# A MoE down-projection: three bfloat16 matmuls per chunk, or one in float32

## The chip, the cores and the metric

The kernel runs on one NeuronCore of a Trainium2 chip. Its engines run side by side, each with its own in-order instruction stream, and wait for each other on semaphores: TensorE (matmuls, from SBUF into PSUM), VectorE, ScalarE, GpSimd, and SyncE, which here only issues transfers. In the profile they are PE, DVE, ACT, POOL and SP; PEld is TensorE's weight load. The metric is the device time of one execution in microseconds (us); less is better.

## The reference

The input is 128 images of 64 x 64 pixels with 128 channels, all float32. A depthwise 3 x 3 convolution and an 8 x 8 mean pool make 64 tokens of 128 numbers from each. Then follow, each added to its input and each on a normalised copy of it: an attention over the 64 tokens of an image, a mixture of experts, a second attention with compressed keys, and a small MLP over the tokens. The change is in the mixture of experts, of which this is the core (`t` holds the tokens, D = 128, F = 512, 2 shared experts and 8 routed ones; the routing gives each token two of these, but all eight are computed and weighted):

```python
hs = gelu(einsum('td,nfd->ntf', t, sw1) + sb1[:, None, :])
shared = einsum('ntf,ndf->td', hs, sw2) + sb2.sum(axis=0)
probs = softmax(t @ gate_w.T + gate_b)
top_v, top_i = top_k(probs, 2)
cw = zeros_like(probs).at[arange(T)[:, None], top_i].add(top_v)
hr = gelu(einsum('td,efd->etf', t, rw1) + rb1[:, None, :])
oe = einsum('etf,edf->etd', hr, rw2) + rb2[:, None, :]
return shared + einsum('etd,te->td', oe, cw)
```

The Gelu is the exact one.

## The kernel before

The images are worked in 16 groups of 8, that is, of 512 tokens. Four stages are pipelined over the groups: `tok` (convolution and pooling), `att` (first attention and routing), `ffn` (the experts) and `sec` (second attention and MLP). Iteration i runs `tok` of group i, `att` of group i-1, `ffn` of i-2 and `sec` of i-3. So iterations 0 to 2 fill the pipeline, 16 to 18 drain it, and those between do all four stages. Twelve of the iterations run as a hardware loop with two iterations in its body; at its end every engine jumps back.

The order of the work on each engine is written out by hand in the table `ORDER`: one string per engine, whose words are pieces such as `up.12`, `pool.3.2` or `att.12`. A word with a prime (`down.38'`) belongs to the iteration before. `iteration` walks through the string and emits each piece with its waits, so every engine executes just this order and a piece that has to wait holds up all that stand behind it.

**The experts.** There are 10 experts with 4 chunks of 128 hidden units each, 40 chunks a group. For chunk q:
- `up.q` on TensorE (L490 to L492) puts the pre-activation [128 x 512 tokens] into one of two banks. Float32 accuracy comes from three bfloat16 products: high times high, low times high, high times low, where high is the value in bfloat16 and low the rest.
- `hidden.q` on ScalarE (L732) takes the Gelu twice from the same bank: once into the bfloat16 tile `hid_h`, once into the float32 tile `hid`.
- `hidden.q` on VectorE (L991), or on GpSimd (L1141) for every fifth chunk, subtracts the two and writes the low part `hid_l`.
- `down.q` on TensorE (L505 to L507) waits for that subtraction (`rest_taken`) and adds three bfloat16 products into `down_bank`, which the four chunks of an expert share (the two shared experts' eight chunks, for the first sum).
- `sum.q` on VectorE (L1001, L1008) takes the bank at an expert's end, with the bias and the token's share of this expert, and GpSimd (L1148) adds it to `moe`. The next expert's first `down` waits for the `sum`.

`hid_h` and `hid_l` are rings of 5 chunks, `hid` a ring of 4. For each routed expert one more matmul (L485) spreads the tokens' shares over the partitions, and ScalarE copies them (L721).

**What lies around it.** `pair` and `inner` on VectorE (L878, L882), `add` on GpSimd (L1133) and `pool` on TensorE (L410, L413, L418) are the pooling of an x tile, `tap` the convolution's 15 steps (L899, the last ones L906), and `out` turns the result (L382). `att.11` computes the routing logits, GpSimd their exponential (L1123), and `att.12` on VectorE is the routing: a chain of 14 dependent small operations (L956 to L986). `low` (L941) splits the normalised tokens into high and low parts, once a group. `turn` and `value` (L575, L584, and L1062 and L1065 on VectorE) are parts of the second attention, `k` in L870 is written by `att.10`.

**Weights.** In iteration 1 all of w1 and w2 (10 slices each of 128 x 512) come in through four staging tiles: GpSimd issues the transfer, ScalarE writes the high part (L657), VectorE the low part (L851). These are the pieces `weights.0` to `weights.19`. The constants come on ScalarE's queue at the start (L637, L639), and each engine waits for all of them at the start of iteration 1.

Of the kernel before, what the change touches and what calls it, by code (L numbers as in the profile page):

```python
# [19 lines left out]
P = 128  # L20
# [17 lines left out]
HIDS = 4  # L38
STAGING = 4
POOL_EVERY = 5  # L40
# [12 lines left out]
        up.0 up.1 down.38' down.39' up.2 up.3 down.0 down.1 up.4 att.1 pool.0.0 pool.0.1 up.5 pre.0 down.2  # L53
        up.6 att.2 down.3 up.7 down.4 att.3 down.5 up.8 down.6 pre.2 pool.0.2 pool.0.3 up.9 up.10 att.4 pre.3
        up.11 down.7 pre.4 up.12 down.8 pre.5 pre.6 pool.1.0 up.13 pool.1.1 down.9 pre.7 up.14 up.15 score.0
        score.1 down.10 down.11 score.2 score.3 up.16 down.12 up.17 pool.1.2 down.13 up.18 down.14 up.19
        pool.1.3 down.15 score.4 up.20 score.5 score.6 down.16 score.7 down.17 up.21 down.18 down.19 up.22
        pool.2.0 pool.2.1 att.7 turn.0 down.20 up.23 turn.1 value.0 att.8 turn.2 value.1 down.21 turn.3
        value.2 up.24 pool.2.2 turn.4 up.25 pool.2.3 down.22 up.26 value.3 down.23 turn.5 att.10 value.4 up.27
        turn.6 value.5 att.11 turn.7 value.6 up.28 value.7 up.29 post.0 down.24 post.1 up.30 down.25 down.26  # L60
        down.27 up.31 pool.3.0 down.28 pool.3.1 up.32 up.33 pool.3.2 pool.3.3 down.29 up.34 att.13 down.30
        up.35 down.31 post.3 up.36 post.4 down.32 up.37 up.38 down.33 down.34 down.35 up.39 post.5 down.36
        down.37 out""",
# [4 lines left out]
        pool.1.0 hidden.13 pre.7 hidden.14 weights.9 hidden.15 inner.1.1 hidden.16 hidden.17 pool.1.2  # L68
        hidden.18 hidden.19 pool.1.3 weights.10 weights.11 hidden.20 weights.12 inner.2.0 att.6 exp hidden.21
        turn.0 weights.13 att.7 weights.14 hidden.22 turn.1 turn.2 hidden.23 pool.2.0 inner.2.1 turn.3  # L70
        hidden.24 hidden.25 turn.4 hidden.26 turn.5 att.10 inner.3.0 turn.6 weights.15 hidden.27 turn.7
        hidden.28 post.0 weights.16 hidden.29 weights.17 hidden.30 pool.2.2 pool.2.3 pool.3.0 hidden.31
        inner.3.1 hidden.32 weights.18 pool.3.2 pool.3.3 hidden.33 hidden.34 hidden.35 post.3 att.13 hidden.36
        hidden.37 post.4 weights.19 hidden.38 hidden.39 post.5 out""",
    dve="""
        pair.0.0 hidden.38' att.0 hidden.0 weights.0 sum.39' hidden.1 att.1 inner.0.0 weights.1 hidden.2
        hidden.3 weights.2 pair.0.1 pre.0 pre.1 hidden.5 hidden.6 pre.2 weights.3 hidden.7 inner.0.1 weights.4
        pair.1.0 pre.5 pre.3 sum.7 weights.5 hidden.8 pre.4 inner.1.0 hidden.10 att.4 pair.1.1 weights.6
        hidden.11 hidden.12 hidden.13 att.5 score.0 weights.7 score.1 sum.11 weights.8 score.2 inner.1.1
        hidden.15 score.3 hidden.16 weights.9 pair.2.0 hidden.17 hidden.18 weights.10 sum.15 tap.0.0 score.4  # L80
        tap.0.1 score.5 tap.0.2 score.6 weights.11 tap.0.3 score.7 tap.0.4 inner.2.0 hidden.20 tap.0.5 sum.19
# [32 lines left out]
def program(nc, x, conv_w, conv_b, wq, bq, wk, bk, gate_w, gate_b, w1, b1, w2, sb2, rb2,  # L114
            swq, swqs, swk, swks, swv, swkc, swvc, swo, comp_gate, sink, tw1, tb1, tw2, tb2,
            ident_c, block_c, cos_c, sin_c, mask1_c, limit_c, place_c, part_c, heads_c, pick_c, tie_c, out):
    with ExitStack() as ctx:
# [174 lines left out]
        def rest_taken(g, q):  # L292

            if q % POOL_EVERY == POOL_EVERY - 1:
                return hid_rest_p, at(hid_rest_p, g, q // POOL_EVERY + 1)
            return hid_rest, at(hid_rest, g, q + 1 - q // POOL_EVERY)


        first = [q + max(0, q // FC - NS + 1) for q in range(CH)]
        def made(n):  # L300
# [968 lines left out]
```

## Time and profile before

| | |
|---|---|
| Median of 3 runs | 2192.52 us (2187.37 to 2193.03) |
| Profiled execution, its own time | 2185.65 us |
| Its span, first to last instruction | 2183.9 us |
| Mean granted TensorE clock in it | 0.956 of 2.4 GHz |
| TensorE busy | 1868.5 us (86%) |
| VectorE busy | 1880.1 us (86%) |
| ScalarE busy | 1331.7 us (61%) |
| GpSimd busy | 1207.4 us (55%) |

Busy time is the time in which an engine had an instruction in work. For TensorE it says less than for the others, since matmuls overlap and the end of each is modelled: the distance from one start to the next tells what a matmul costs in a row of them. An idle stretch is put down to what ended it ("<- DVE part L1008"), and "issue" is time in which the engine waited for nothing that the profile shows. Idle time costs something only on the engine that sets the pace.

### The profile page before, as it was taken

How to read it: one execution, taken by the hardware profiler on the slowest of the kernel's cores; microseconds unless marked ns; L12 is line 12 of the kernel's file. 1: busy time of each engine (PE TensorE's matmuls, PEld its weight loads, DVE VectorE, ACT ScalarE, POOL GpSimd, SP SyncE). 2: the span in 40 equal slices, each digit the busy share in tenths (PEclk: the TensorE clock that was granted, in tenths of full speed). 3: DMA queues.
4: the chain of work that ended last, by engine and by line, in shares of the span. 5: the costliest groups of instructions: out<-in, count | busy, mean ns of one | idle time of the engine just before them, and what ended most of it. 6: DMA issues, size and time to landing. Idle time of an engine off the chain costs nothing.

```text
span 2183.9 us, 38353 instructions
## 1 busy us (share of the span) xinstructions
PE 1868.5 (86%) x12224; PEld 1066.0 (49%) x12224; DVE 1880.1 (86%) x3524; ACT 1331.7 (61%) x2319; POOL 1207.4 (55%) x796
## 2 busy tenths in 40 slices
PE   2355889898988989798998989888998989899986
PEld 2344545455454545455454555545454555544444
DVE  1667899999999999899998989989998989987762
ACT  0234767666675766567675757657675756768752
POOL 1244557574755657575663757466565647554532
PEclk9999999999999999899998989999998989999996
DMA  5664534243343434334333424333343433200000
GB/s 181 250 241 183 193 123 155 114 159 151 121 160 117 155 121 155 122 145 165 121 129 137 155 94 160 150 122 150 125 155 112 164 122 124 109 6 1 5 6 5
DMA packets 33616, 282.00 MB, mean 129 GB/s; under 512 B 5470, under 2 KB 15649, under 8 KB 17020
## 3 DMA queue, kind: packets, MB, share of 16 engines
q1 hardware_dynamic: 18432, 268.44, 32.1%
q10 hardware_dynamic: 13372, 5.66, 0.9%
q0 software_dynamic: 1600, 5.24, 0.6%
q8 instruction: 112, 1.84, 0.3%
q14 instruction: 100, 0.82, 0.1%
HBM read 275.14 MB, written 4.19 MB: 128 GB/s over the span
## 4 chain that ended last, share of the span: by engine, by line
PE 40%; DVE 35%; issue 16%; DMA 2%; POOL 2%; ACT 2%; ACTq 1%; DVEq 1%; POOLq 0%
DVE taps L899 7%; DVE hid_l L991 7%; DVE xbuf L878 5%; PE pool_bank L413 4%; PE hid_bank L490 3%; PE down_bank L505 3%; PE hid_bank L492 3%; PE hid_bank L491 3%; PE down_bank L507 2%; PE down_bank L506 2%; PE sec_bank L528 2%; PE pool_bank L418 2%; PE sec_bank L544 2%; DMA xbuf<-in_x 2%; DVE k L870 2%
## 5 line engine op out<-in xcount | busy, mean ns | idle before, releaser
L732 ACT ACTIVATE hid_h<-hid_bank,b_s 128x512 bf16<-128x512 f32 x640 | 439.3, 686 | 280.9 <-PE hid_bank L492 221.9
L991 DVE TENSOR_TENSOR hid_l<-hid,hid_h 128x512 bf16<-128x512 f32 x512 | 498.3, 988 | 21.3 <-ACT hid L732 20.9
L1133 POOL TENSOR_TENSOR xbuf<-xbuf 128x512 f32<-128x512 f32 x256 | 359.8, 1405 | 266.1 <-DVE xbuf L878 257.2
L732 ACT ACTIVATE hid<-hid_bank,b_s 128x512 f32<-128x512 f32 x640 | 437.3, 683 | 0.0
L1141 POOL TENSOR_TENSOR hid_l<-hid,hid_h 128x512 bf16<-128x512 f32 x128 | 201.1, 1571 | 201.7 <-ACT hid L732 201.7
L1148 POOL TENSOR_TENSOR moe<-moe,part 128x512 f32<-128x512 f32 x128 | 196.6, 1536 | 179.9 <-DVE part L1008 178.1
L490 PE MATMUL hid_bank<-x2h,w1h 128*128 128x512 bf16 x640 | 253.8, 396 | 28.6 <-issue 17.7
L505 PE MATMUL down_bank<-hid_h,w2h 128*128 128x512 bf16 x640 | 252.5, 395 | 27.2 <-DVE part L1008 20.4
L899 DVE SCALAR_TENSOR_TENSOR taps<-pooled_s,tapw,taps 128x256 f32<-128x256 f32 (+1 forms) x416 | 269.6, 648 | 3.5
L878 DVE TENSOR_TENSOR xbuf<-xbuf 128x1536 f32<-128x1536 f32 x128 | 229.8, 1795 | 32.0 <-DMA xbuf<-in_x 23.6
L491 PE MATMUL hid_bank<-x2h,w1l 128*128 128x512 bf16 x640 | 250.9, 392 | 0.0
L492 PE MATMUL hid_bank<-x2l,w1h 128*128 128x512 bf16 x640 | 250.5, 391 | 0.0
L506 PE MATMUL down_bank<-hid_h,w2l 128*128 128x512 bf16 x640 | 250.4, 391 | 0.0
L507 PE MATMUL down_bank<-hid_l,w2h 128*128 128x512 bf16 x640 | 249.8, 390 | 0.0
L1175 POOL TENSOR_TENSOR keys_h<-keys,heads 128x632 f32<-128x632 f32 x128 | 206.9, 1640 | 4.7 <-PE sec_bank L564 3.4
L410 PE MATMUL pool_bank<-block_b,xbuf 128*128 128x48 bf16 x1024 | 50.5, 191 | 133.7 <-DVE xbuf L882 92.4
L413 PE MATMUL pool_bank<-block_sum,xbuf 128*128 128x48 f32 x1024 | 161.9, 308 | 0.0
L676 ACT ACTIVATE pooled_s<-pool_bank 128x384 f32<-128x384 f32 x192 | 90.4, 491 | 115.0 <-PE pool_bank L413 110.4
L1114 POOL TENSOR_TENSOR rs<-ve,power 128x4 f32<-128x4 f32 x64 | 80.8, 1262 | 139.0 <-DVE ve L865 136.4
L418 PEld LDWEIGHTS pool_bank<-block_sum,xbuf 128*128 128x128 f32 x1024 | 143.9, 211 | 11.2 <-issue 1.0
L413 PEld LDWEIGHTS pool_bank<-block_sum,xbuf 128*128 128x128 f32 x1024 | 148.1, 223 | 0.0
L418 PE MATMUL pool_bank<-block_sum,xbuf 128*128 128x48 f32 x1024 | 142.4, 288 | 0.0
(180 smaller groups left out, 3329.3 us busy)
## 6 DMA issues: line engine op xcount, KB each, us to landing
xbuf<-in_x SPq DMA_DIRECT2D x128, 2048.0 KB, 7.3
out<-h ACTq DMA_DIRECT2D x16, 256.0 KB, 2.2
hid<-in_w POOLq DMA_DIRECT2D x10, 256.0 KB, 4.4
part<-in_w POOLq DMA_DIRECT2D x10, 256.0 KB, 6.4
keys_h<-in_limit_c ACTq DMA_DIRECT2D x1, 167.5 KB
tw_s<-in_tw ACTq DMA_DIRECT2D x2, 64.0 KB
share_b<-in_pick_c ACTq DMA_DIRECT2D x1, 96.0 KB
ident<-in_ident_c ACTq DMA_DIRECT2D x1, 64.0 KB, 12.2
```

The costliest lines, as they stand in the source:

```text
L413: mm = nc.tensor.matmul(view[:, 1, :, side[bx]], blocks[v][:, bx, 0, :], block_sum[:], start=True, stop=True)
L418: mm = nc.tensor.matmul(view[:, :, v, side[bx]], blocks[v][:, bx, 7, :], block_sum[:], start=True, stop=True)
L490: nc.tensor.matmul(bank[:], w1h[:, e, cols], x2h[b][:], start=True, stop=False)
L491: nc.tensor.matmul(bank[:], w1l[:, e, cols], x2h[b][:], start=False, stop=False)
L492: nc.tensor.matmul(bank[:], w1h[:, e, cols], x2l[b][:], start=False, stop=True).then_inc(hid_done, 1)
L505: nc.tensor.matmul(down_bank[:], w2h[:, e, cols], hid_h[:, r, :], start=begin, stop=False)
L506: nc.tensor.matmul(down_bank[:], w2l[:, e, cols], hid_h[:, r, :], start=False, stop=False)
L732: nc.scalar.activation(dst[:, r, :], hid_bank[n % 2][:], ACT.Gelu, bias=b1_s[:, q:q + 1]) \
L878: nc.vector.tensor_tensor(v[:, :, 1:6:2, :], v[:, :, 1:6:2, :], v[:, :, 2:7:2, :], ALU.add) \
L899: nc.vector.scalar_tensor_tensor(dst, src, w, dst, ALU.mult, ALU.add).then_inc(tapped, 1)
L991: nc.vector.tensor_tensor(hid_l[:, q % RING, :], hid[:, q % HIDS, :], hid_h[:, q % RING, :], ALU.subtract).then_inc(hid_rest, 1)
L1133: nc.gpsimd.tensor_tensor(v[:, :, 1, :], v[:, :, 1, :], v[:, :, 2 * k + 3, :], ALU.add) \
```

## The change

Down becomes one native float32 matmul per chunk, `hid` times `w2_s`, both float32. The second Gelu and the tiles `hid_h` and `hid_l` go, with the subtractions on VectorE and GpSimd; `hid` becomes a ring of 5. `down.q` waits for the Gelu itself (`hid_made`). The weights w2 are no longer split: they come as they are in one transfer of 128 x 5120 float32 (2.6 MB), the last of the constants on ScalarE's queue, and the pieces `weights.10` to `weights.19` are gone. From `ORDER` only the words `hidden.*` of VectorE and GpSimd and those ten `weights.*` are taken out; the rest stands in the same order, and TensorE's string has the same words as before.

```diff
-HIDS = 4
 STAGING = 4
-POOL_EVERY = 5
 RING = 5
...
     dve="""
-        pair.0.0 hidden.38' att.0 hidden.0 weights.0 sum.39' hidden.1 att.1 inner.0.0 weights.1 hidden.2
+        pair.0.0 att.0 weights.0 sum.39' att.1 inner.0.0 weights.1 weights.2 pair.0.1 pre.0 pre.1 pre.2 weights.3
...
-        w2h, w2l = sb("w2h", [P, NX, F], bf16), sb("w2l", [P, NX, F], bf16)
+        w2_s = sb("w2_s", [P, NX, F])
...
-        hid = sb("hid", [P, HIDS, F])
-        hid_h, hid_l = sb("hid_h", [P, RING, F], bf16), sb("hid_l", [P, RING, F], bf16)
+        hid = sb("hid", [P, RING, F])
...
-                 (tb1_s, tb1), (tb2_s, tb2)]
+                 (tb1_s, tb1), (tb2_s, tb2), (w2_s, w2)]
...
-        lots = [(w1, w1h, w1l, e) for e in range(NX)] + [(w2, w2h, w2l, e) for e in range(NX)]
+        lots = [(w1, w1h, w1l, e) for e in range(NX)]
...
-                eng.wait_ge(*rest_taken(g, q))
+                eng.wait_ge(hid_made, at(hid_made, g, first[q] + 1))
...
-                nc.tensor.matmul(down_bank[:], w2h[:, e, cols], hid_h[:, r, :], start=begin, stop=False)
-                nc.tensor.matmul(down_bank[:], w2l[:, e, cols], hid_h[:, r, :], start=False, stop=False)
-                nc.tensor.matmul(down_bank[:], w2h[:, e, cols], hid_l[:, r, :], start=False, stop=end) \
+                nc.tensor.matmul(down_bank[:], w2_s[:, e, cols], hid[:, r, :], start=begin, stop=end) \
                   .then_inc(hid_used, 1)
...
-                if q >= HIDS:
-                    eng.wait_ge(*rest_taken(g, q - HIDS))
-                elif after(g, 1):
-                    eng.wait_ge(*rest_taken(g - 1, CH + q - HIDS))
-                for dst, r in ((hid_h, q % RING), (hid, q % HIDS)):
-                    nc.scalar.activation(dst[:, r, :], hid_bank[n % 2][:], ACT.Gelu, bias=b1_s[:, q:q + 1]) \
-                      .then_inc(hid_made, 1)
+                nc.scalar.activation(hid[:, q % RING, :], hid_bank[n % 2][:], ACT.Gelu, bias=b1_s[:, q:q + 1]) \
+                  .then_inc(hid_made, 1)
...
-            def hidden(g, q):
-
-                eng.wait_ge(hid_made, at(hid_made, g, made(first[q] + 1)))
-                nc.vector.tensor_tensor(hid_l[:, q % RING, :], hid[:, q % HIDS, :], hid_h[:, q % RING, :],
-                                        ALU.subtract).then_inc(hid_rest, 1)
```

How it moves the instructions is seen best on TensorE and VectorE. First TensorE before, with down.25, down.26 and down.27, then up.31 (L490 to L492):

```order
L505 MATMUL down_bank<-hid_h,w2h 128x512 [waits hid_rest]
L506 MATMUL down_bank<-hid_h,w2l 128x512
L507 MATMUL down_bank<-hid_l,w2h 128x512
L505 MATMUL down_bank<-hid_h,w2h 128x512 [waits hid_rest]
L506 MATMUL down_bank<-hid_h,w2l 128x512
L507 MATMUL down_bank<-hid_l,w2h 128x512
L505 MATMUL down_bank<-hid_h,w2h 128x512 [waits hid_rest]
L506 MATMUL down_bank<-hid_h,w2l 128x512
L507 MATMUL down_bank<-hid_l,w2h 128x512
L490 MATMUL hid_bank<-x2h,w1h 128x512 [waits hid_made]
L491 MATMUL hid_bank<-x2h,w1l 128x512
L492 MATMUL hid_bank<-x2l,w1h 128x512
```

The same place after, where the down matmul is L481 and up is L466 to L468:

```order
L481 MATMUL down_bank<-hid,w_s 128x512 [waits hid_made] x3
L466 MATMUL hid_bank<-x2h,w1h 128x512 [waits hid_made]
L467 MATMUL hid_bank<-x2h,w1l 128x512
L468 MATMUL hid_bank<-x2l,w1h 128x512
L386 MATMUL pool_bank<-block_b,xbuf 128x3x16 [waits pooled_read,inner_low,x_in0]
L386 MATMUL pool_bank<-block_b,xbuf 128x3x16 x7
L389 MATMUL pool_bank<-block_sum,xbuf 128x3x16 x4
```

Nine down matmuls in bfloat16 became three in float32, and they wait for the Gelu (`hid_made`) instead of the subtraction (`hid_rest`).

VectorE before, from the shared experts' `sum.7` (L1001) to the row maximum of the first attention (L925):

```order
L1001 TENSOR_SCALAR moe<-down_bank,sb_sum 128x512 [waits moe_turned,hid_used]
L991 TENSOR_TENSOR hid_l<-hid,hid_h 128x512 [waits hid_made]
L1035 TENSOR_TENSOR keys_h<-sec_bank,cos 128x512 [waits rope_added,rope_done]
L1035 TENSOR_TENSOR keys_h<-sec_bank,sin 128x512 [waits rope_done]
L882 TENSOR_TENSOR xbuf<-xbuf 128x4x128 [waits inner_high]
L991 TENSOR_TENSOR hid_l<-hid,hid_h 128x512 [waits hid_made]
L921 TENSOR_TENSOR s<-att_bank,mask 128x512 [waits s1_done]
L878 TENSOR_TENSOR xbuf<-xbuf 128x4x3x128 [waits x_in1]
L991 TENSOR_TENSOR hid_l<-hid,hid_h 128x512 [waits hid_made] x3
L925 TENSOR_REDUCE nmax<-s 128x4 [waits s1_masked]
L1054 TENSOR_REDUCE m<-sec_bank 128x4 [waits scored]
```

And after, from the same `sum.7` (now L964), with the maximum at L894:

```order
L964 TENSOR_SCALAR moe<-down_bank,sb_sum 128x512 [waits moe_turned,hid_used]
L995 TENSOR_TENSOR keys_h<-sec_bank,cos 128x512 [waits rope_added,rope_done]
L995 TENSOR_TENSOR keys_h<-sec_bank,sin 128x512 [waits rope_done]
L851 TENSOR_TENSOR xbuf<-xbuf 128x4x128 [waits inner_high]
L890 TENSOR_TENSOR s<-att_bank,mask 128x512 [waits s1_done]
L847 TENSOR_TENSOR xbuf<-xbuf 128x4x3x128 [waits x_in1]
L894 TENSOR_REDUCE nmax<-s 128x4 [waits s1_masked]
L1014 TENSOR_REDUCE m<-sec_bank 128x4 [waits scored]
```

Five subtractions are gone from between, and what stood behind them moves up in the same order.

## Rows read from the trace of the kernel before

**Rows 1.** Page, part 1: engine, busy us, share of the span, instructions.
```profile
PE 1868.5 (86%) x12224; PEld 1066.0 (49%) x12224; DVE 1880.1 (86%) x3524; ACT 1331.7 (61%) x2319; POOL 1207.4 (55%) x796
```

**Rows 2.** Timeline of VectorE, its `low` pieces: start us, us, engine, line, operation.
```profile
192.53 0.69 DVE L941 TENSOR_TENSOR x2l<-x1t,x2h 128x512 bf16<-128x512 f32 x1
...
288.23 0.69 DVE L941 TENSOR_TENSOR x2l<-x1t,x2h 128x512 bf16<-128x512 f32 x1
...
1908.59 0.69 DVE L941 TENSOR_TENSOR x2l<-x1t,x2h 128x512 bf16<-128x512 f32 x1
```

**Rows 3.** Busy time by windows: length, busy us (instructions) of each engine, clock, DMA.
```profile
288.20:1908.60 1620.40, 1475.43 (x9923) 831.98 (x9922) 1520.86 (x2822) 1064.49 (x1858) 985.53 (x624) 0.96 0.36 136
1167.64:1296.74 129.10, 117.55 (x764) 66.52 (x764) 116.32 (x218) 81.87 (x143) 75.19 (x49) 0.92 0.35 134
1296.74:1419.57 122.83, 112.52 (x764) 63.71 (x764) 117.14 (x218) 81.99 (x143) 76.16 (x49) 0.97 0.37 140
1921.89:2019.76 97.87, 91.93 (x567) 45.83 (x568) 72.94 (x172) 72.05 (x123) 47.33 (x32) 1.00 0.01 4
2019.76:2108.66 88.90, 86.29 (x525) 40.76 (x524) 60.12 (x117) 66.77 (x108) 39.21 (x30) 1.00 0.01 4
```

**Rows 4.** Waits of TensorE, 288.2 to 1908.6 us: total us, times, longest.
```profile
PE pool_bank L410 <- DVE xbuf L882: 41.6, 13, 3.4
PE pool_bank L382 <- DVE cols L906: 24.3, 13, 1.9
PE down_bank L505 <- DVE part L1008: 18.1, 36, 1.2
PE hid_bank L490 <- issue: 17.7, 5, 3.7
PE sec_bank L584 <- DVE x L1065: 13.3, 13, 1.0
PE att_bank L382 <- DVE k L870: 12.9, 13, 1.0
```

**Rows 5.** Page, part 5: groups: busy us, mean ns, idle before.
```profile
L991 DVE TENSOR_TENSOR hid_l<-hid,hid_h 128x512 bf16<-128x512 f32 x512 | 498.3, 988 | 21.3 <-ACT hid L732 20.9
...
L732 ACT ACTIVATE hid<-hid_bank,b_s 128x512 f32<-128x512 f32 x640 | 437.3, 683 | 0.0
L1141 POOL TENSOR_TENSOR hid_l<-hid,hid_h 128x512 bf16<-128x512 f32 x128 | 201.1, 1571 | 201.7 <-ACT hid L732 201.7
```

**Rows 6.** Timeline of TensorE, around three down chunks.
```profile
1015.58 0.38 PE L505 MATMUL down_bank<-hid_h,w2h 128*128 128x512 bf16 x1
...
1017.52 0.38 PE L490 MATMUL hid_bank<-x2h,w1h 128*128 128x512 bf16 x1
```

**Rows 7.** Timeline of TensorE, float32 matmuls of 512 columns.
```profile
2035.20 1.02 PE L528 MATMUL sec_bank<-x3t,second_q 128*128 128x512 f32 x2
2036.06 1.02 PE L528 MATMUL sec_bank<-x3t,second_qs 128*128 128x512 f32 x2
2036.91 0.38 PE L490 MATMUL hid_bank<-x2h,w1h 128*128 128x512 bf16 x1
```

**Rows 8.** Groups by shape, weight loads.
```profile
L528 PEld LDWEIGHTS sec_bank<-x3t,second_qs 128*128 128x128 f32 x32 | 6.4, 199 | 8.2 <-issue 8.2
```

**Rows 9.** Timeline of VectorE, around the routing chain.
```profile
1018.88 0.75 DVE L1008 SCALAR_TENSOR_TENSOR part<-down_bank,rb_s,share_b 128x512 f32<-128x512 f32 x1
1019.54 0.18 DVE L956 TENSOR_REDUCE esum<-ez 128x4 f32<-128x32 f32 x1
...
1026.61 0.69 DVE L882 TENSOR_TENSOR xbuf<-xbuf 128x512 bf16<-128x512 f32 x1
```

**Rows 10.** Timeline of TensorE, the wait behind it.
```profile
1027.43 0.37 PE L410 MATMUL pool_bank<-block_b,xbuf 128*128 128x48 bf16 x8 [3.37 <-DVE xbuf L882]
```

**Rows 11.** Page, part 6: DMA issues: KB each, us to landing.
```profile
xbuf<-in_x SPq DMA_DIRECT2D x128, 2048.0 KB, 7.3
```

**Rows 12.** Groups by shape, VectorE, the low parts of w2.
```profile
L851 DVE TENSOR_TENSOR w2l<-part,w2h 128x512 bf16<-128x512 f32 x6 | 4.1, 687 | 1.7 <-ACT w2h L657 1.7
```

## What I predict, before the run

> **What bounds the kernel now.** I read the page's first part, then the busy time by windows, then the waits of TensorE, then the timelines of TensorE and VectorE around the longest of these waits.
>
> The page shows two engines at 86%, TensorE and VectorE [rows 1]. The steady part runs from one `low` piece (L941) at 288.23 us to another at 1908.59 us [rows 2]; 13 periods lie between, so a period is 1620.4/13 = 124.65 us. In it VectorE is busy 1520.86/13 = 117.0 us, TensorE 1475.43/13 = 113.5, ScalarE 81.9, GpSimd 75.8 [rows 3]. VectorE has 7.6 us left, most of it in gaps between dependent instructions: it is the saturated engine. TensorE idles 11.15 us in a period. 127.9 of its 145 us of idle time have a name in six groups, and five of them, 110.2 us, end on VectorE [rows 4]. So VectorE sets the pace and TensorE is close behind: whatever takes load from the first and gives it to the second ends on TensorE soon. The granted clock is 0.96 in this stretch, that is, part of it is spent at 1.2 GHz instead of 2.4. A period without the loop's jump shows 0.97 and 112.52 us of TensorE, one with the jump 0.92 and 117.55 [rows 3]: one point of clock is worth about 5.03/5 = 1.0 us of TensorE's busy time.
>
> **What goes.** Of VectorE, the 512 `hid_l` subtractions: 498.3 us, 31.1 in each of the 16 groups. Of ScalarE, one of two Gelu per chunk: 437.3 us, 27.3 a group. Of GpSimd, 128 subtractions, 201.1 us, 12.6 a group [rows 5]. A period's loads become 117.0 - 31.1 = 85.9 us on VectorE, 54.6 on ScalarE, 63.2 on GpSimd. None of it is worth its own size: these three engines stop being the bound, and TensorE has only 11.15 us of idle time to give.
>
> **What comes.** Each down chunk was three bfloat16 matmuls of 512 columns. Three chunks in a row start at 1015.58 and the next work at 1017.52, which is 1.94/3 = 0.647 us a chunk [rows 6]. (A record's own 0.38 is longer than its slot of 0.215, since its end is modelled 0.165 behind.) A float32 matmul of the same shape stands in the trace as two records; two such matmuls start at 2035.20 and 2036.06, and the next work at 2036.91: 0.855 to 0.86 each [rows 7]. So a chunk costs 0.86 - 0.647 = 0.213 us more, 8.5 us a group of 40 chunks, 136 us over 16 groups at the full clock, and twice that where the clock is at 1.2 GHz.
>
> The float32 weight loads take 199 ns on average [rows 8], and each of the two pairs of rows 7 runs at 0.43 us a record with its load inside. The Trainium skill, "TensorE: Matmul & The Clock Gate", section "Weight-path perf modes", says that the fast weight load does not apply to float32 weights, which speaks against this change. Were the loads not covered, two of them would add 0.4 us a chunk, or 256 us in all; by the spacing of rows 7 they add nothing, and the sum takes nothing.
>
> **What TensorE gets back, per period.** Down now waits for a Gelu and no longer for a subtraction behind it in VectorE's queue. The waits [rows 4], one by one:
> - `pool_bank` on L882, 3.2 us. `inner.3.1` stands on VectorE behind the routing chain (L956 to L986), and that chain behind `sum.27` [rows 9]. `sum.27` needs down.27, whose slot ended at 1017.52 [rows 6] and moves 0.85 us later with the four longer downs 24 to 27; as the sum started only at 1018.88 it need start no later. Then the chain runs 7.1 us (1019.54 to 1026.61) and L882 0.7. TensorE has 1.1 us more work (five downs) before it asks. One GpSimd subtraction that shared the time is gone; I put the chain 1.0 us shorter at most. From 3.37 [rows 10] a wait of 1.3 to 2.3 is left; I keep 1.9 of 3.2.
> - `pool_bank` on L906, 1.9 us. The taps are done earlier, but L906 also stands behind `post.5`, which TensorE itself releases two downs before. I keep 0.7.
> - `down_bank` on the sums, 1.4 us: every sum has up or pool work between; I keep 0.1. L1065 and L870 (`k`), 1.0 each: VectorE was late by `hidden.21` to `hidden.23`, which go; I keep 0.
> - The jump of the loop ("issue"), 1.4 us, stays. The unnamed and small rest, 1.3 us: I keep 0.75.
>
> That leaves 4.85 us, so 6.3 less than 11.15. Both ends: nothing goes (0), or all but the jump (9.8). Five or six waits a period fewer also spare their modelled tail of 0.165, 0.9 us. The clock: the drop behind the 3.4 us wait may go, the one behind the jump stays; from 0.96 to between 0.98 and 0.99 I take 2.5 us; ends 0 and 4.0.
>
> A period: 8.5 - 6.3 - 0.9 - 2.5 = -1.2 us. Times 13: -15.6 us.
>
> **Outside the steady part.** Two late iterations run without the token stage. TensorE is busy 91.93 of 97.87 us in one and 86.29 of 88.90 in the other, at full clock [rows 3]: 5.9 and 2.6 us of idle time against 8.5 us more work each. I let 2.6 and 1.4 of it go: +5.9 and +7.1 us. The first expert iteration has more idle time (VectorE sets it): I take -1.5. At the start, ten w2 slices no longer pass through staging, which frees 10 x 0.68 us of VectorE [rows 12]; but w2 (2.6 MB) now goes in one transfer behind the constants, beside the x loads, which take 7.3 us for 2.1 MB [rows 11]. Full cost 7.3 x 2.6/2.1 = 9 us, full gain 6.8: I take 0, ends -7 and +9.
>
> **The sum,** on the profiled execution's own 2185.65 us: -15.6 + 5.9 + 7.1 - 1.5 = -4.1, about 2182 us, which I forecast. That execution is 0.3% under the median of the runs, 2192.52, and within 0.1% of their lowest, 2187.37. The measurement can tell a difference of about 0.3%, 6.6 us, from none.
>
> **Rivals.**
> 1. *TensorE streams on.* Nearly all waits but the jump go and the clock stays at 2.4 GHz between jumps. For it: five of the six wait groups end on VectorE, which loses a quarter of its load. Against it: the routing chain and `post.5` hang on TensorE's own progress. Per period 8.5 - 8.8 - 1.2 - 3.2 = -4.7, times 13 = -61, and +8 outside: 2133. Half way to it is 2158.
> 2. *The routing wait stays* (slower). The chain starts at `sum.27`, whose down.27 moves with TensorE; no gap closes, the 3.2 us wait stays whole, and the clock falls behind it as before. That takes back 1.3 and 2.5 us: a period is 8.5 - 5.0 - 0.9 = +2.6, times 13 = +34, and +11.5 outside: 2231. It decides from the point where waits and clock together return less than 8.5 - 0.9 us a period. For it: the two iterations without the token stage have VectorE at three quarters and still wait for such chains. Against it: VectorE's backlog is in the wait too.
> 3. *The start pays.* The w2 transfer delays the x loads by its whole 9 us and the gain does not come: 2192, no change.
> 4. *TensorE has room and the passes cost nothing,* so the period falls by VectorE's 31.1 us: 2185.65 - 13 x 31.1 = 1781. Rows 6 speak against it: the records follow each other in 0.215 us without a gap. The Trainium skill, "Trainium Kernel Development and Optimization", section "Performance Expectations", calls matmul busy time a bad measure of how near TensorE is to its roofline and names the share of weight loads as a good one. That is 832/1620 = 51% here; by it there would be room.
>
> **Chances.** The forecast's case, about even, 0.46 (its own range 2160 to 2205: faster 0.21, same 0.15, slower 0.10); rival 1 with what lies half way, 0.25, faster; rival 2 0.24, slower; rival 3 0.04 (same 0.03, slower 0.01); rival 4 0.01. Faster 0.21 + 0.25 + 0.01 = 0.47, same 0.18, slower 0.35. The range takes in most of rival 1, down to 2138, and rival 2, up to 2235; a tenth of each side is left out.
>
> **What would show it.** After: 640 pairs of float32 down records, two to a chunk, 0.86 us from chunk to chunk, and no `hid_l`. VectorE near 86 us a period and under 75% busy, ScalarE near 55. TensorE idle 4 to 6 us a period, its first two groups still L882 (near 25 us in 13 periods) and L906 (near 9), no wait on `hid_l`, almost none on the sums. A clock of 0.98. I am wrong in the size of the passes if chunks follow at more than 0.9 us, wrong in the waits if TensorE's idle time stays above 8 us a period, and wrong at the start if the first `low` piece, which the trace of before has at 192.5 us, comes more than 5 us earlier or later.

## The result and the profile after

The changed kernel takes 2208.43 us (median of 4 runs, 2207.12 to 2211.14) against 2189.94 in the same comparison: a ratio of 1.0091, 95% interval 1.0072 to 1.011. It is 0.9% slower where I forecast 0.4% faster; 2208 lies in the range. The profiled executions differ a little more, 2207.8 against 2183.9 us of span, +23.9.

The page, part 1 and the two groups of the change, against [rows 1] and [rows 5]:

```profile
PE 1988.7 (90%) x11584; PEld 1116.8 (51%) x11584; DVE 1389.0 (63%) x3002; ACT 974.1 (44%) x1669; POOL 942.3 (43%) x658
...
L481 PE MATMUL down_bank<-hid,w_s 128*128 128x512 f32 x1280 | 666.3, 622 | 2.2 <-DVE part L971 2.2
L701 ACT ACTIVATE hid<-hid_bank,b_s 128x512 f32<-128x512 f32 x640 | 437.8, 686 | 513.0 <-PE hid_bank L468 426.6
```

The load moved as the diff says: VectorE from 86% to 63%, TensorE to 90%. The timeline of VectorE, its `low` pieces (start, length), against [rows 2]:

```profile
190.56 0.69 DVE L910 TENSOR_TENSOR x2l<-x1t,x2h 128x512 bf16<-128x512 f32 x1
...
282.15 0.69 DVE L910 TENSOR_TENSOR x2l<-x1t,x2h 128x512 bf16<-128x512 f32 x1
...
1918.16 0.69 DVE L910 TENSOR_TENSOR x2l<-x1t,x2h 128x512 bf16<-128x512 f32 x1
```

The second `low` comes 6.1 us earlier than before, the 13 periods take 1636.0 us instead of 1620.4 (+15.6), the end behind them 289.6 instead of 275.3 (+14.3). Together +23.8. A period is 125.85 us, 1.2 more than before, where I forecast 1.2 less. Busy time by windows (length, then TensorE, its loads, VectorE, ScalarE, GpSimd, clock), against [rows 3]:

```profile
282.15:1918.16 1636.01, 1572.12 (x9405) 872.50 (x9404) 1119.04 (x2406) 777.72 (x1338) 769.05 (x520) 0.97 0.36 135
1170.43:1300.16 129.73, 123.37 (x725) 68.47 (x724) 84.94 (x186) 59.89 (x103) 59.05 (x40) 0.95 0.35 133
1047.57:1170.43 122.86, 119.13 (x725) 66.25 (x724) 86.35 (x186) 59.86 (x103) 59.18 (x40) 0.99 0.37 140
1931.10:2037.15 106.05, 103.36 (x531) 51.52 (x530) 46.22 (x141) 50.67 (x83) 32.57 (x24) 0.97 0.01 3
2037.15:2132.84 95.69, 94.69 (x485) 44.29 (x484) 32.69 (x84) 45.02 (x67) 25.68 (x22) 1.00 0.01 4
```

Per period TensorE is busy 120.9 us (113.5 before) and idle 4.9 (11.15 before). A period without the jump is as long as before, 122.9 against 122.8, with 6.6 us more work in it. One with the jump is 129.7 against 129.1 in the pair shown; over all five, 129.9 against 127.7 by the starts of `low`. The two iterations without the token stage are 8.2 and 6.8 us longer, most of the 8.5 of the passes. TensorE's waits in the steady part, against [rows 4]:

```profile
PE pool_bank L386 <- DVE xbuf L851: 35.0, 13, 3.2
PE hid_bank L466 <- issue: 17.9, 5, 3.7
PE pool_bank L358 <- DVE cols L875: 9.1, 13, 0.7
PE down_bank L481 <- DVE part L971: 1.6, 4, 0.4
```

Of the six groups of before two are gone, the sums' is down to a tenth, the taps' from 24.3 to 9.1. The wait for the routing chain kept 2.7 of its 3.2 us. Around it, the timeline of VectorE, against [rows 9]:

```profile
1144.76 0.75 DVE L971 SCALAR_TENSOR_TENSOR part<-down_bank,rb_s,share_b 128x512 f32<-128x512 f32 x1
1145.43 0.18 DVE L925 TENSOR_REDUCE esum<-ez 128x4 f32<-128x32 f32 x1
...
1147.16 1.42 DVE L933 TENSOR_TENSOR s<-prob 128x256 f32<-128x256 f32 x1
1148.51 1.49 DVE L934 TENSOR_TENSOR s<-prob 128x256 f32<-128x256 f32 x1
...
1152.62 0.69 DVE L851 TENSOR_TENSOR xbuf<-xbuf 128x512 bf16<-128x512 f32 x1
```

and what TensorE does meanwhile (against [rows 10]), with the busy time of 2 us behind the wait, whose last figures are clock, DMA share and GB/s:

```profile
1153.44 0.37 PE L386 MATMUL pool_bank<-block_b,xbuf 128*128 128x48 bf16 x8 [2.98 <-DVE xbuf L851]
```

```profile
1155.00:1157.00 2.00, 2.00 (x5) 0.46 (x3) 1.72 (x6) 0.83 (x2) 0.00 (x0) 0.50 0.67 139
```

The chain takes 7.2 us as before (7.1). TensorE stands 2.98 us for it, and behind that its granted clock is 0.50, that is 1.2 GHz, as it was behind the 3.37 us wait of before.

So it is in nine of the 13 periods, with waits of 2.6 to 3.2 us. In the other four the chain takes 6.6 us and TensorE waits 1.98, about what I forecast. The clock falls there too:

```profile
1283.17 0.37 PE L386 MATMUL pool_bank<-block_b,xbuf 128*128 128x48 bf16 x8 [1.98 <-DVE xbuf L851]
```

```profile
1284.80:1286.80 2.00, 2.00 (x5) 0.46 (x3) 1.78 (x6) 0.76 (x2) 0.00 (x0) 0.50 0.73 188
```

### The profile page after: what moved, and what is told of

It reads as the page before. It is cut to its first block, busy times and chain, and to the rows that moved or that the text cites. A ratio compares the mean times of both kernels' runs of the same rounds, so it can differ in the third digit from the quotient of the medians.

```text
span 2207.8 us, 34437 instructions
## 1 busy us (share of the span) xinstructions
PE 1988.7 (90%) x11584; PEld 1116.8 (51%) x11584; DVE 1389.0 (63%) x3002; ACT 974.1 (44%) x1669; POOL 942.3 (43%) x658
## 4 chain that ended last, share of the span: by engine, by line
PE 78%; DVE 10%; issue 6%; DMA 2%; ACTq 1%; POOL 1%; ACT 1%; DVEq 0%; POOLq 0%
PE down_bank L481 24%; PE hid_bank L466 7%; PE hid_bank L468 6%; PE hid_bank L467 6%; PE pool_bank L389 5%; PE sec_bank L538 4%; PE pool_bank L394 4%; PE sec_bank L558 3%; PE sec_bank L549 2%; PE sec_bank L502 2%; DMA xbuf<-in_x 2%; PE sec_bank L518 2%; PE sec_bank L520 2%; PE hid_bank L461 2%; PE sec_bank L358 1%
## 5 line engine op out<-in xcount | busy, mean ns | idle before, releaser
L481 PE MATMUL down_bank<-hid,w_s 128*128 128x512 f32 x1280 | 666.3, 622 | 2.2 <-DVE part L971 2.2
L1093 POOL TENSOR_TENSOR xbuf<-xbuf 128x512 f32<-128x512 f32 x256 | 332.4, 1298 | 341.0 <-DVE xbuf L847 332.0
L1102 POOL TENSOR_TENSOR moe<-moe,part 128x512 f32<-128x512 f32 x128 | 183.6, 1434 | 441.7 <-DVE part L971 440.2
L481 PEld LDWEIGHTS down_bank<-hid,w_s 128*128 128x128 f32 x1280 | 230.0, 195 | 154.3 <-issue 111.0
L466 PE MATMUL hid_bank<-x2h,w1h 128*128 128x512 bf16 x640 | 253.1, 395 | 18.4 <-issue 17.9
L468 PE MATMUL hid_bank<-x2l,w1h 128*128 128x512 bf16 x640 | 251.4, 393 | 0.0
L971 DVE SCALAR_TENSOR_TENSOR part<-down_bank,rb_s,share_b 128x512 f32<-128x512 f32 x128 | 96.1, 751 | 237.9 <-PE down_bank L481 237.7
L1014 DVE TENSOR_REDUCE m<-sec_bank 128x4 f32<-128x320 f32 x128 | 62.4, 488 | 151.3 <-PE sec_bank L538 148.6
L389 PE MATMUL pool_bank<-block_sum,xbuf 128*128 128x48 f32 x1024 | 153.1, 297 | 0.0
L1074 POOL TENSOR_TENSOR rs<-ve,power 128x4 f32<-128x4 f32 x64 | 68.8, 1075 | 171.2 <-DVE ve L834 171.1
L394 PE MATMUL pool_bank<-block_sum,xbuf 128*128 128x48 f32 x1024 | 141.6, 286 | 0.0
L389 PEld LDWEIGHTS pool_bank<-block_sum,xbuf 128*128 128x128 f32 x1024 | 139.5, 211 | 0.0
L466 PEld LDWEIGHTS hid_bank<-x2h,w1h 128*128 128x128 bf16 x640 | 66.7, 104 | 141.9 <-issue 114.2
L1083 POOL TENSOR_TENSOR ez<-euler,lg 128x32 f32<-128x32 f32 x16 | 90.4, 5653 | 108.3 <-DVE lg L919 108.3
```

What stands on the lines that cost most here:

```text
L389: mm = nc.tensor.matmul(view[:, 1, :, side[bx]], blocks[v][:, bx, 0, :], block_sum[:], start=True, stop=True)
L394: mm = nc.tensor.matmul(view[:, :, v, side[bx]], blocks[v][:, bx, 7, :], block_sum[:], start=True, stop=True)
L466: nc.tensor.matmul(bank[:], w1h[:, e, cols], x2h[b][:], start=True, stop=False)
L468: nc.tensor.matmul(bank[:], w1h[:, e, cols], x2l[b][:], start=False, stop=True).then_inc(hid_done, 1)
L481: nc.tensor.matmul(down_bank[:], w2_s[:, e, cols], hid[:, r, :], start=begin, stop=end) \
L1093: nc.gpsimd.tensor_tensor(v[:, :, 1, :], v[:, :, 1, :], v[:, :, 2 * k + 3, :], ALU.add) \
```

## The experiments

Each kernel is timed against the kernel before on the same chip; the ratio is to that kernel. The kernel before took 2188 to 2191 us in these comparisons, so differences of a few us between two kernels from different ones say little.

**1. The two halves of the change.** `relief_alone` is the kernel before with

```diff
-                for dst, r in ((hid_h, q % RING), (hid, q % HIDS)):
-                    nc.scalar.activation(dst[:, r, :], ..., ACT.Gelu, ...).then_inc(hid_made, 1)
+                nc.scalar.activation(hid_h[:, q % RING, :], ..., ACT.Gelu, ...).then_inc(hid_made, 1)
-                nc.tensor.matmul(down_bank[:], w2h[:, e, cols], hid_l[:, r, :], start=False, stop=end)
+                nc.tensor.matmul(down_bank[:], w2h[:, e, cols], hid_h[:, r, :], start=False, stop=end)
```

and no `hidden` pieces on VectorE and GpSimd. The third matmul reads the high part once more, so the low part is left out of the result.

> One Gelu per chunk (written as bfloat16) and no subtraction, but the down product still in three bfloat16 matmuls; the low part of the hidden values is left out, its matmul reads the high part instead. Theory 1 (the float32 passes cost 0.213 us a chunk plus about 0.1 where their weight loads are not covered, and all of it lies on TensorE's path): against the changed kernel's 2208 us, 640 x 0.213 = 136 and 13 to 19 us of weight loads less, 2055 to 2075; TensorE's idle time near 5 us a period. Theory 2 (a faster TensorE only waits longer for the routing chain and the other small chains, so the relief itself was worth little): 2110 to 2150, TensorE's idle time 9 us a period or more.

Measured: 2101.58 us, ratio 0.9606 (0.9583 to 0.9628). `passes_alone` is the other half, the kernel before with

```diff
-                nc.tensor.matmul(down_bank[:], w2h[:, e, cols], hid_h[:, r, :], start=begin, stop=False)
-                ...
+                nc.tensor.matmul(down_bank[:], w2_s[:, e, cols], hid[:, r, :], start=begin, stop=end)
```

a ring of five in `hid`, w2 loaded as in the changed kernel, and the wait for the subtraction kept.

> The float32 down matmuls with both Gelus and all subtractions kept; down still waits for its subtraction, whose result nobody reads. Theory 1 (passes on the path, minus what hides in waits for VectorE): 136 plus 13 to 19 us more than before less up to 60 that hides in the 11 us a period of idle time, 2270 to 2340; TensorE's idle time 7 us a period or more. Theory 2 (the relief did nothing for the time, the changed kernel is as slow as its passes alone): within 10 us of the changed kernel, 2200 to 2220.

Measured: 2256.9 us, ratio 1.0315 (1.0292 to 1.0339), just under the expected range, with 6.4 us of idle time a period instead of 7 or more. The steady parts by windows, and the first wait of each:

```profile
282.50:1827.34 1544.84, 1461.11 (x9923) 839.33 (x9922) 1120.82 (x2405) 774.59 (x1338) 773.42 (x520) 0.96 0.38 143
```

```profile
PE pool_bank L410 <- DVE xbuf L877: 42.1, 13, 3.5
```

```profile
288.47:1965.86 1677.39, 1594.69 (x9395) 880.04 (x9394) 1500.49 (x2822) 1064.13 (x1857) 974.80 (x624) 0.96 0.35 132
```

```profile
PE pool_bank L410 <- DVE xbuf L880: 33.2, 13, 3.1
```

Four times stand in a square: 2188 with neither half, 2102 with the relief, 2257 with the passes, 2208 with both. The relief is worth 87 us beside bfloat16 and 49 beside float32; the passes cost 69 where VectorE is the bound and 107 where it is not. The halves do not add: each was partly hidden by what the other takes away. `relief_alone` lies between the two theories (2075 and 2110): its idle time is 6.4 us a period, and half of it, 3.2, is the routing wait, which the relief did not touch at all.

**2. Cover for the weight loads.** Ten places of TensorE's order, of which one stretch, each version in one line:

```diff
-        up.13 pool.1.1 down.9 pre.7 up.14 up.15 score.0 score.1 down.10 down.11 score.2 score.3 up.16 down.12
+        up.13 down.9 pool.1.1 pre.7 up.14 down.10 up.15 score.0 score.1 up.16 down.11 score.2 score.3 up.17 down.12
```

> The changed kernel with TensorE's order altered in ten places, so that a float32 down stands behind an up or another down where it stood behind pool, score, value or transposing matmuls. Theory A (a float32 weight load that no 512-column matmul covers costs 0.07 to 0.10 us, some twelve chunks a period): mean down slot falls and the time by 12 to 20 us, to 2188 to 2196. Theory B (the longer slots come with the short matmuls themselves and stay in the sum wherever the down stands): within 5 us of 2208. A new wait that costs more than 3 us a period would show as TensorE idle time above 8 us.

Measured: 2222.29 us, ratio 1.0159 (1.0139 to 1.018): slower than the changed kernel, outside both. What the theory looked at is there. In the changed kernel, TensorE's timeline shows a down behind transposes of 128 columns (L549, at 1116.46) and one behind value matmuls of 17 columns (L558, at 1121.04):

```profile
1116.90 1.02 PE L481 MATMUL down_bank<-hid,w_s 128*128 128x512 f32 x2
1117.76 0.38 PE L466 MATMUL hid_bank<-x2h,w1h 128*128 128x512 bf16 x1
...
1121.61 1.12 PE L481 MATMUL down_bank<-hid,w_s 128*128 128x512 f32 x2
1122.57 0.60 PE L549 MATMUL sec_bank<-ident,e 128*80 128x128 f32 x4
```

0.86 us from start to start the first time, as also behind matmuls of 512 columns, and 0.96 the second. Some ten downs a period are longer like the second, 1.0 us together. In `cover` nearly all take 0.86, but its waits grew: the routing wait from 2.7 to 3.0 us a period, a new one of an up for a Gelu by 0.8.

`cover_inner` lays the same order on `inner_first` (below), where no routing wait disturbs:

> inner_first with TensorE's order of cover, and hidden.31 ahead of pool.3.0 on ScalarE (in cover an up waited 0.8 us for it). Theory A (uncovered float32 weight loads cost some 1.2 us a period; cover lost only by the waits it made, which end with the moved inner.3.1): 8 to 18 us less than inner_first's 2136, 2118 to 2128. Theory B (covering the downs only hands the cost to the other short matmuls): within 5 us of 2136.

Measured: 2148.06 us, ratio 0.9798 (0.978 to 0.9816), 12 us above `inner_first` and outside both theories. By the ratios it is 7 us (0.9798 against 0.9766, whose intervals just touch); its periods without the jump are nearly all 118.9 us against 117.95. Its window and waits in a period without the jump:

```profile
1009.96:1129.03 119.07, 115.63 (x714) 66.55 (x725) 86.45 (x187) 59.72 (x104) 59.18 (x40) 1.00 0.39 149
```

```profile
PE att_bank L444 <- DVE parts L956: 1.3, 1, 1.3
PE pool_bank L359 <- DVE cols L876: 0.7, 1, 0.7
```

With two more of 0.3 and 0.2, 2.5 of 119.07 us are waits, 116.6 are not; in `inner_first` (next) 117.2 are not. So the cover saves 0.6 us and buys 1.8 us of waits. Part of what the downs save comes back in another slot: the 64 pool matmuls of L390 take 8.0 us a period from start to start, and 7.3 in `inner_first` (L389). The load is real and small; this order is not the way to get it.

**3. The routing wait by order.** `inner_first`:

```diff
-        turn.7 hidden.28 post.0 hidden.29 hidden.30 pool.2.2 pool.2.3 pool.3.0 hidden.31 inner.3.1 hidden.32
+        turn.7 hidden.28 post.0 hidden.29 hidden.30 pool.2.2 pool.2.3 inner.3.1 pool.3.0 hidden.31 hidden.32
-        post.1 tap.0.14 post.2 sum.27 att.12 inner.3.1 tap.1.0
+        post.1 tap.0.14 post.2 sum.27 inner.3.1 att.12 tap.1.0
```

> The changed kernel with inner.3.1 ahead of pool.3.0 on ScalarE and ahead of the routing chain att.12 on VectorE. Theory A (the 2.7 us a period wait of pool.3.3 for VectorE, and the clock that falls behind it, are a matter of order alone): 2.7 to 4.5 us a period less, 16 places, 2140 to 2170. Theory B (another wait takes its place, att.13 for the chain that is now 0.7 us later): at most 1 us a period, 2190 to 2210.

Measured: 2135.86 us, ratio 0.9766 (0.9747 to 0.9786): 72 us under the changed kernel, theory A and 4 us below its range. The steady part and a period without the jump, with that period's only wait:

```profile
278.23:1848.86 1570.63, 1540.73 (x9402) 861.16 (x9401) 1116.83 (x2405) 779.59 (x1337) 770.91 (x520) 0.99 0.37 141
1004.54:1122.49 117.95, 117.20 (x725) 65.65 (x724) 85.69 (x186) 60.08 (x103) 59.32 (x40) 1.00 0.38 145
```

```profile
PE pool_bank L358 <- DVE cols L875: 0.7, 1, 0.7
```

TensorE's idle time falls from 4.9 to 2.3 us a period, and its busy time for the same instructions from 120.9 to 118.5. These 2.4 us are the clock (and 0.17 of one modelled tail).

`before_inner` makes the same two moves in the kernel before.

> The kernel before, with the same two moves of inner.3.1 (ahead of pool.3.0 on ScalarE, ahead of att.12 on VectorE). Theory 1 (before, VectorE is the bound with 117 us of work in 124.6, so a wait removed on TensorE comes back elsewhere): 10 to 30 us less than before, 2160 to 2180, so that the same move is worth less here than the 72 us it was worth in the changed kernel; the change as a whole then gains 1 to 2%. Theory 2 (the wait and its clock are a matter of order alone, whatever VectorE's load): the same 65 to 75 us, 2115 to 2125, and the change stays about 0.9% slower.

Measured: 2169.64 us, ratio 0.9904 (0.9889 to 0.9919), 21 us less: theory 1. The taps' wait is as before, 23.9 us. The routing wait comes back at other things VectorE owes, a sum and an x (L869; L870 before, with 4.6 us):

```profile
PE down_bank L504 <- DVE part L1007: 23.0, 23, 3.2
PE sec_bank L381 <- DVE x L869: 20.6, 13, 1.9
```

So with these moves in both, the change makes the kernel 1.4% faster (0.9766/0.9904 = 0.986; 0.983 to 0.990 by the ends of the two intervals), and without them 0.9% slower.

`relief_inner` is `relief_alone` with the two moves, to price the passes where nearly nothing waits.

> relief_alone (one Gelu, no subtraction, three bfloat16 matmuls per down chunk; the low part of the hidden values is left out) with the two moves of inner.3.1. It prices the passes where hardly a wait is left. Theory 1 (float32 costs 0.213 us a chunk and nothing else): 136 us less than inner_first's 2136, 1995 to 2005. Theory 2 (float32 also costs its uncovered weight loads): 150 to 160 less, 1976 to 1986. Theory 3 (the faster TensorE meets other waits): 2020 or more.

Measured: 2032.05 us, ratio 0.9292 (0.927 to 0.9314): theory 3 by the time. By a period without the jump the price is seen bare:

```profile
1187.77:1299.27 111.50, 107.71 (x753) 62.58 (x765) 86.23 (x186) 59.91 (x104) 59.80 (x40) 1.00 0.40 154
```

```profile
PE pool_bank L381 <- DVE cols L900: 1.2, 1, 1.2
PE att_bank L381 <- DVE x L864: 0.8, 1, 0.8
PE att_bank L466 <- DVE parts L980: 0.6, 1, 0.6
```

with one more of 0.2 on a sum. 111.5 - 2.8 = 108.7 against 117.95 - 0.7 = 117.25: the float32 passes cost 8.55 us a group of 40 chunks, 0.214 each. The forecast had 0.213. That holds the longer downs of experiment 2 and still comes to 0.214, since bfloat16 pays too, in another slot: from start to start, 64 pool matmuls (L412 in `relief_inner`, L389 in `inner_first`) take 8.5 us a period in `relief_inner` and 7.3 in `inner_first`.

**4. What makes the chain long.** `pool_held` changes one thing on GpSimd in the changed kernel:

```diff
+                    if not isinstance(g, int) or g + 2 < NG:
+                        eng.wait_ge(gate_step, at(gate_step, g + 2, 10))
                     nc.gpsimd.tensor_tensor(h3b[:], h3[:], tb2_s...
```

> The changed kernel with GpSimd's post.1, and the sums behind it, held back until the large steps of the routing chain are done on VectorE. The chain takes 7.2 us, of which 4.2 are three operations (L929, L933, L934) beside which GpSimd works. Theory A (GpSimd slows them; alone they would take 1.1): the chain is 3 us shorter, the 2.7 us wait of pool.3.3 goes and the clock stays up, 60 to 72 us less, 2136 to 2150. Theory B (these operations are slow by their own access pattern): the chain stays over 6.5 us, 2200 to 2215.

Measured: 2202.14 us, ratio 1.0052 (1.0035 to 1.0069). Time and chain length are theory B's, but its reason is not: L933 and L934 do get short. Timeline of VectorE, then of GpSimd:

```profile
1146.45 0.18 DVE L925 TENSOR_REDUCE esum<-ez 128x4 f32<-128x32 f32 x1
...
1147.10 0.42 DVE L933 TENSOR_TENSOR s<-prob 128x256 f32<-128x256 f32 x1
...
1150.20 1.18 DVE L947 CAST parts<-share 128x32 bf16<-128x32 f32 x1
...
1151.64 1.13 DVE L951 CAST parts<-rest 128x32 bf16<-128x32 f32 x1
...
1153.14 0.69 DVE L851 TENSOR_TENSOR xbuf<-xbuf 128x512 bf16<-128x512 f32 x1
```

```profile
1148.86 1.26 POOL L1139 TENSOR_TENSOR h<-h,tb_s 128x512 f32<-128x512 f32 x1 [2.58 <-DVE s L939]
1150.08 2.66 POOL L1102 TENSOR_TENSOR moe<-moe,part 128x512 f32<-128x512 f32 x2
```

L933 falls from 1.42 to 0.42 us, but two casts of 32 columns behind it grow from 0.18 to 1.2 and 1.1. The second ends at 1152.77, GpSimd's pair of sums at 1152.74. The slowing moved with GpSimd's work; the chain is still 6.7 us. The wait here was 2.06 us, near the 1.9 that I had forecast for the changed kernel, and the clock fell behind it all the same:

```profile
1156.00:1158.00 2.00, 2.00 (x8) 0.63 (x6) 1.96 (x7) 0.63 (x2) 0.00 (x0) 0.50 0.92 254
```

`pool_held_long` waits for the chain's last step:

```diff
-                        eng.wait_ge(gate_step, at(gate_step, g + 2, 10))
+                        eng.wait_ge(gate_step, at(gate_step, g + 2, 17))
```

> As pool_held, but GpSimd is held until the routing chain's last step. In pool_held L933 fell from 1.30 to 0.42 us and the chain still took 6.7, since the small steps behind, beside GpSimd's moved work, grew from 0.2 to 1.2. Theory A (GpSimd's work beside VectorE is the whole of what lengthens the chain): the chain is 4 to 4.5 us, the wait of pool.3.3 below 1 us, the clock stays up behind it, 2135 to 2155. Theory B (the chain ends earlier but another engine, the sums or the inner copy, ends the wait at the same place): a wait over 2 us stays, the clock falls again, 2195 to 2210.

Measured: 2139.35 us, ratio 0.9776 (0.9751 to 0.9802), theory A. The chain on VectorE, and a period without the jump:

```profile
1116.89 0.18 DVE L925 TENSOR_REDUCE esum<-ez 128x4 f32<-128x32 f32 x1
...
1120.91 0.69 DVE L851 TENSOR_TENSOR xbuf<-xbuf 128x512 bf16<-128x512 f32 x1
```

```profile
1008.64:1126.93 118.29, 116.16 (x714) 65.70 (x725) 84.18 (x187) 59.94 (x104) 59.46 (x40) 1.00 0.38 146
```

The chain takes 4.0 us instead of 7.2 (L929 0.19, L933 0.43, L934 0.42), the wait is gone, the clock stays at 1.00. One semaphore wait on an engine that is busy 43% of the time is worth 69 us. `inner_held` puts both remedies together.

> inner_first with GpSimd held until the chain's last step. inner_first has no wait left for the chain, so a shorter chain has nothing to give: 2130 to 2140 by both theories, unless the GpSimd work that is now late (h3b, two sums) makes waits of its own, then 2145 or more.

Measured: 2139.66 us, ratio 0.9782 (0.9758 to 0.9806): nothing more to have, as expected. Two different edits, one of order and one of contention, end at the same time, and both remove the same wait.

**5. The jump.** `no_jump` and `no_jump_before` write the steady loop out:

```diff
-                with eng.Fori(0, (NG - LAG_ALL - 1) // 2) as j:
-                    ...
+                for i in range(NG + LAG_ALL):
+                    iteration(i, i)
```

> The changed kernel with its 12 steady iterations written out instead of a loop of six jumps. Theory A (a jump and the low clock behind it make a period 7.0 us longer, 129.9 against 122.9): six times 7.0 less, 2160 to 2172, periods all near 122.9. Theory B (the longer period is the second iteration's own, or code loading costs as much as the jump): 2195 to 2215.

> The kernel before with its 12 steady iterations written out. Theory A (a jump period is 4.9 us longer than the others, 127.7 against 122.8, less than in the changed kernel, so part of the result is the jump's): six times 4.9 less, 2155 to 2165, and the changed kernel without jumps is 0 to 12 us slower instead of 19. Theory B (the jump costs both the same): the difference between the two stays 19 us, 2145 or 2190.

Measured: 2172.78 us (0.992, 0.9905 to 0.9936) and 2160.55 (0.987, 0.9853 to 0.9887). Without jumps the changed kernel is 12 us slower instead of 18. So the jumps cost the changed kernel 36 us and the kernel before 30: theory A, for the changed kernel 1 us beyond its edge. The loop runs its body six times, but the traces show TensorE's wait for the jump only five times (17.7 us before, 17.9 after, all in the steady part), so it is 6 to 7 us a jump. `inner_no_jump` joins the moves and the written-out loop.

> inner_first with the 12 steady iterations written out. Theory A (the two gains are separate: 72 us from the order, 36 from the jumps): 2095 to 2105. Theory B (part of the jump's cost was a clock already low behind the routing wait, or the jump lets other engines catch up): 2110 to 2125.

Measured: 2113.03 us, ratio 0.9646 (0.9619 to 0.9672), the fastest kernel here that computes the whole, 4.3% under the changed one. It takes back 23 us of the jumps' 36, theory B in size but for another reason. From the seventh of the 13 periods on, every second one is 2.3 us longer than those between. One of each:

```profile
868.14:986.11 117.97, 116.00 (x714) 65.80 (x725) 85.62 (x187) 60.12 (x103) 59.74 (x40) 1.00 0.38 146
986.11:1106.80 120.69, 118.72 (x712) 67.65 (x723) 84.53 (x186) 60.00 (x103) 60.31 (x40) 0.97 0.37 141
```

The second has no wait that the first has not; its clock falls in the middle of value and transposing pieces. Four such periods, and three between them that are 0.4 longer, make 12 us; without them, by this estimate, the time would be 2101 and in theory A's range. What starts the fall is left open.

**6. The start.** `w2_late`:

```diff
+                if n == len(lots) - 1:
+                    eng.dma_start(w2_s[:], w2).then_inc(w2_in, 16)
```

> The changed kernel with w2's transfer issued by GpSimd behind the last slice of w1, waited for only before the first up. Theory A (w2's 2.6 MB beside the first x loads cost 1.3 to 1.5 us there): first low near 189, 1 to 2 us less in the whole, not to be told from 2208 by the times. Theory B (the start's constants, which all engines wait for, hang on w2): first low 4 us or more earlier.

Measured: 2214.52 us, ratio 1.011 (1.0093 to 1.0127), not to be told from the changed kernel. Both theories failed: the first pool pieces do come 1.4 us earlier (50.69 against 52.09), but the first `low` is at 193.79 instead of 190.56. The transfer, 12.9 us long, now runs beside later x loads: between 130 and 160 us they take 10.8 us (7.3 in the changed kernel), and one wait of the pool pieces grows from 7.43 to 11.92 us.

## Why the prediction was wrong, step by step

- *What goes.* Right for VectorE: 86.1 us a period against 85.9. ScalarE has 59.8 instead of 54.6, since the two Gelus of a chunk overlapped in the trace by 0.11 us, 4.4 us in 40 chunks, which the group's 27.3 counts twice. GpSimd has 59.2 instead of 63.2, since what stayed there got shorter too (the adds into `xbuf` from 1.41 to 1.29 us, those into `moe` from 1.56 to 1.47). Neither changed the time, as far as the waits show.
- *What comes: the passes.* Right. 8.5 us a period forecast, 8.55 measured in experiment 3. The weight loads were the doubt I had. The Trainium skill, "TensorE: Matmul & The Clock Gate", section "Weight-path perf modes", has float32 weights without the fast load, and the trace agrees: 195 ns a load on L481 against 104 on L466. It shows where nothing long covers the load, by 0.10 us, and came to nothing against bfloat16.
- *What TensorE gets back: idle time.* Right in the sum, 4.9 us against 4.85, by two errors that cancel. The small waits went more fully than I allowed (the rest 0.0 instead of 0.75), and L906's successor kept 0.7 as forecast. The routing wait kept 2.7 instead of 1.9.
- *The routing wait, 1.9 of 3.2 us kept.* It kept 2.7, by two faults. I took one GpSimd subtraction away from beside the chain and credited VectorE with up to a microsecond. The chain stayed at 7.2 us in nine periods and took 6.6 in four, since a sum on GpSimd moved up to the subtraction's place. `pool_held_long` shows that GpSimd's work beside it is worth 3.2 us to the chain. And TensorE comes to its wait only 0.5 us later, where I had 1.1: 11.48 us behind the start of down.24, and 10.97 before. 0.36 us of that difference went where it had waited for `sum.27` ahead of down.28.
- *The clock.* This is the step that failed, and the term that turned the sign. I credited 2.5 us a period, on the ground that a wait of 1.3 to 2.3 us may leave the clock up. Busy time rose by 7.4; the passes are 8.55 of it and the spared tails -1.1 (113.5 to 112.4 in `relief_alone`, forecast -0.9), which leaves next to nothing for the clock. It fell behind all 13 routing waits: behind those of 2.98 us, and behind the four of 1.98, where the wait was what I had forecast; so the error in the wait alone does not explain it. The 2.5 us themselves were the right size: they appear, as 2.4, once the wait is gone and not merely shorter. The sum 8.5 - 6.3 - 0.9 - 2.5 without its last term is +1.3 a period, and +1.2 was measured.
- *Outside.* The tail: +14.3 us against +13.0. The start: the second `low` 6.1 us earlier, against 1.5. The two terms that I set to 0 give little: w2's transfer costs 1.3 us at the first x loads, the ten slices gain more, and the first `low` is 2.0 us earlier. The rest is the relief: `relief_alone`, which keeps the ten slices, has its second `low` at 282.50, and `passes_alone`, which has lost them, at 288.47 (before: 288.23).
- *Rivals.* Rival 2, the routing wait stays, had the mechanism and named the right place; its +34 us for the steady part was too much because the other waits still went. Rival 1 needed the same wait gone. `inner_first`, 2136, comes near its 2133, but partly by luck: the steady part fell by 50 us where it had 61, and outside it nothing was lost where it had 8. Rival 4 rested on the share of weight loads as the measure of room. That share is 872.5/1636 = 53% now, with TensorE streaming 96% of the time, so here it was no measure of room.

My case against rival 2 was "VectorE's backlog is in the wait too". It was not: `relief_alone` takes the whole backlog away and the wait stays 3.2 us.

## What to carry to other kernels

When load is moved from a full engine to the next fullest, price the gain at what that one (here TensorE) idles, and look for the wait that does not hang on load: a chain of dependent steps keeps its length when its engine is relieved. Count a clock term in full only if the wait goes: shorter waits of 1.98 and 2.06 us brought the fall all the same. Before giving up a change that came out even, remove the longest wait left: the same change lost 0.9% with it and won 1.4% without it (0.9766 against 0.9904).

## What the runs showed of the hardware that I had not expected

- Most VectorE steps of the chain that ran beside a GpSimd operation lengthened by up to 1.1 us each, whatever their own size: a comparison of 256 columns from 0.42 to 1.49 us, a cast of 32 columns from 0.18 to 1.18, each to about the end of a GpSimd operation. Not all did: L925 and L927 (4 columns) keep 0.18 us in the changed kernel beside GpSimd's L1074. The Trainium skill, "SBUF — State Buffer", section "SBUF: two separate sides", says that a GpSimd operation and a VectorE operation with two SBUF inputs, or in a mode that uses two ports, take one shared pair of ports as an exclusive lock for the whole instruction, and that the other blocks. The rows of experiment 4 agree with such blocking; which lock it is, no run here shows. Work on GpSimd was therefore not free beside this chain: moved behind it in `pool_held_long`, the same work made no wait of TensorE.
- A granted clock of 0.50 followed waits of TensorE of 1.98, 2.06, 2.98 and 3.37 us. The length of the wait does not decide it alone: in `pool_held` the clock stayed at 1.00 behind two waits of 2.47 and 2.48 us (that end at 901 and 1659 us), and in the kernel before behind one of 1.89 on the taps. The latter, with the window behind it:

```profile
1298.47 0.65 PE L382 MATMUL pool_bank<-ident,cols 128*128 128x128 f32 x4 [1.89 <-DVE cols L906]
```

```profile
1298.50:1306.00 7.50, 6.35 (x30) 2.80 (x31) 7.42 (x16) 5.95 (x10) 5.82 (x4) 1.00 0.12 36
```

  In `inner_no_jump` it fell with no wait ahead of it.
- A jump of the loop costs 6 to 7 us (30 and 36 us for five), of which TensorE's wait is up to 3.7 us. Behind each of them its granted clock fell to 0.50.
